# Decoder layer on one core: x1 of batches 1 to 3 transposed by DMA instead of TensorE

## The chip, the core and the metric

The kernel runs on one core of a Trainium2 chip. Its engines work side by side and wait for each other through semaphores: TensorE (PE) multiplies matrices and loads their stationary operands (PEld), VectorE (DVE), ScalarE (ACT) and GpSimd (POOL) work element by element, SyncE (SP) starts most of the DMAs. SBUF is the memory on the core, 128 partitions wide; PSUM holds TensorE's results. The metric is the time of one launch on the device in microseconds (us); lower is better. All times in the rows are counted from the start of the profiled span.

## The reference, cut to what matters

```
x1 = layernorm(x + attention_like(x))                       # (4, 512, 512) float32
xq = quant_dequant(x1)          # one scale for the whole tensor, rounded to fp8 (e4m3) values
cq = quant_dequant(ctx)
x2 = layernorm(x1 + einsum('bmk,bkn->bmn', xq, cq) + mask)  # the "cross" stage
mlp = silu(x2 @ gate_w) * (x2 @ up_w) @ down_w              # 512 -> 2048 -> 512
out = layernorm(x2 + mlp + experts(x2))                     # 8 of 1024 experts for each token
```

## The kernel before

There are 4 batches of 512 tokens; a batch is four tiles of 128 tokens by 512 features, tile i of batch b is `tile(4b + i)` of `xall`, which stays in SBUF in float32, tokens on partitions. Every stage writes its result over the same tile.

The program has two blocks. The first makes x1 for all batches and the scale of the quantisation. The second starts near 234 us; the change lies in its first 100 us.

**The cross stage.** `cross` multiplies the rounded x1 of a batch by the rounded ctx; the contraction runs over features, so the stationary operand has to have features on partitions. Before the change PE transposes x1 in float32 into the four PSUM banks gu0 to gu3 (function `transposes`, L1553; batch 0 in the first block), signals `x1t_mm`, and ACT copies each tile out of PSUM, multiplied by the scale, into `y_q` (`scaled`, L1187, signal `y_scaled`), and then writes a rounding magnitude `m_q` (L1189, signal `y_done`). DVE rounds with two instructions (`quantise`, L1293 and L1295) and writes bf16 values into `x_q`, already in the features' layout, signal `q_done`. PE's `cross` (L1561) waits for `q_done` of each tile.

**The mask.** POOL adds the mask to x1 by an accumulating DMA into `xall` (`add_mask`, L152). It may do this only when nobody needs x1 without the mask any more, so it waits for `x1t_mm` of that batch. POOL works in the order of its code: in turn n the addition for batch n + 2 stands between `low_h(n, 0)` and `power(n + 1)`, which makes rstd for the layernorm (L1102).

**x2 and the feed-forward product.** DVE adds the cross product to x1 (`residual`, L1303, L1305), finds the variance (L1310, L1312), and after POOL's rstd normalises (L1322). PE transposes x2 (the same `transposes`, signal `x2t_mm`), ACT and DVE split it into a high and a low part (L1195, L1328). The gate and up products use three PE products per pair of operands (L1541 to L1543), written in PSUM banks gu0, gu1 for the first half c = 0 of the hidden columns and gu2, gu3 for the second. ACT takes silu of gate (L1201), DVE multiplies by up (`middle`, L1334), ACT rounds (h_hi, L1207), POOL takes the remainder (h_lo, L1096), and PE makes the down product.

**The loop.** For n = 0, 1, 2 PE does: gate and up of batch n, half 0; cross of batch n + 1; the first eight transposes of x1 of batch n + 2; gate of half 1; the other eight; up of half 1; `down_early(n, 0)`; the sixteen transposes of x2 of batch n + 1; `down_early(n, 1)`. For n = 2 there is no batch n + 2 and no x1 transposes. Everything is written out by hand in this order; nothing reorders it when it runs. SP's order there is: store x2 of batch 0, load weights, store x2 of batch 1, load weights, and so on.

Of the kernel before, what the change touches and what calls it, by code (L numbers as in the profile page):

```python
# [16 lines left out]
BF16 = mybir.dt.bfloat16  # L17
I32 = mybir.dt.int32
U32 = mybir.dt.uint32
ALU = mybir.AluOpType  # L20
# [3 lines left out]
P = 128  # L24
B, S, D = 4, 512, 512
KC = D // P
# [63 lines left out]
def decoder_layer(nc, x, ctx, mask, w_in, b_in, w_out, b_out, gamma, beta, w_q, keys, down_embed, up_embed,  # L90
# [14 lines left out]
    with ExitStack() as whole:  # L105
        def sem(name):
            return whole.enter_context(nc.semaphore(name))
# [41 lines left out]
        def add_mask(b):  # L149

            nc.gpsimd.wait_ge(x1t_mm, TB * (b + 1))
            nc.gpsimd.dma_start(xall[:, b * TB * D:(b + 1) * TB * D].rearrange("p (t n) -> p t n", t=TB), mask[b, 0].partition_broadcast(P).unsqueeze(1).broadcast_to([P, TB, D]),  # L152
                                accum_op=ALU.add).then_inc(xm_in[b], 16)
# [5 lines left out]
        table_in = sem("table_in")  # L159
        x1t_mm = sem("x1t_mm")  # L160
        first_steps = []

        with ExitStack() as first:
# [69 lines left out]
            def tile(j):  # L233
                return xall[:, j * D:(j + 1) * D]
# [680 lines left out]
        with ExitStack() as second:  # L915
# [33 lines left out]
            m_q = [half[:, i * D:(i + 1) * D] for half in (scratch[:, 7 * D:8 * D].bitcast(BF16), x2_tok[0][:].bitcast(BF16)) for i in range(2)]  # L949
            x_q = scratch[:, 4 * D:6 * D].bitcast(BF16).rearrange("p (t c n) -> p t c n", t=TB, c=KC)  # L950
            ctx_f32 = ctx_q[:].bitcast(F32)
            qT = ctx_f32[:, 0:NT * P]
# [10 lines left out]
            def h_of(n):  # L963
                return h_end if n == UNITS - 1 else (h_hi, h_lo)

            key_in, x2_out, row_in, x2_in = sem("key_in"), [sem(f"x2_out{b}") for b in range(B)], sem("row_in"), [sem("x2_in0"), sem("x2_in1")]
            y_scaled, y_done, q_done, cross_mm, z2_done, v3_ready, r3_ready, x2_done, x2t_mm, h2_done, l2_done = (
                sem(n) for n in ("y_scaled", "y_done", "q_done", "cross_mm", "z2_done", "v3_ready", "r3_ready", "x2_done", "x2t_mm", "h2_done", "l2_done"))
            gate_mm, up_mm, silu_done, mid_done, hhi_done, hlo_done, down_mm, acc_done = (
                sem(n) for n in ("gate_mm", "up_mm", "silu_done", "mid_done", "hhi_done", "hlo_done", "down_mm", "acc_done"))  # L970
            query_mm, query_out, route_mm, route_out, soft_in, exp_done = (sem(n) for n in ("query_mm", "query_out", "route_mm", "route_out", "soft_in", "exp_done"))
            idx_ready, row_got, dot_done, gate_done, coef_done, pick_done = sem("idx_ready"), [sem(f"row_got{k}") for k in range(TOPK)], sem("dot_done"), sem("gate_done"), sem("coef_done"), sem("pick_done")
            key_zero, rows_clear = sem("key_zero"), sem("rows_clear")
            var_out, rstd_out, y_out, stored = sem("var_out"), sem("rstd_out"), sem("y_out"), sem("stored")
            block = second.enter_context(nc.Block())

            def tile(j):
                return xall[:, bass.ds(j * D, D)]

            def x1t_bank(b, i):  # L980

                return i if b < 2 else i % 2


# [23 lines left out]
            def _(sp):  # L1008
# [13 lines left out]
                def store_x2(b):  # L1022
                    sp.wait_ge(x2_done, TB * (b + 1))
                    sp.dma_start(x2_dram[:, b * TB * D:(b + 1) * TB * D], xall[:, b * TB * D:(b + 1) * TB * D]).then_inc(x2_out[b], 16)

                def load_x2(t):

                    if t >= 2:
                        sp.wait_ge(dot_done, (TOPK + 1) * (t - 1))
                    sp.dma_start(x2_tok[t % 2][:], x2_dram[:, t * D:(t + 1) * D]).then_inc(x2_in[t % 2], 16)  # L1030
# [7 lines left out]
                load(2, 0, 2)  # L1038
                load(3, 0, 3)
                store_x2(0)  # L1040
                load(4, 1, 0)
                store_x2(1)
                load(5, 1, 1)
                store_x2(2)
                load(6, 1, 2)
# [121 lines left out]
            def _(act):  # L1167
# [12 lines left out]
                def scaled(b, tiles):  # L1180
                    for i in tiles:

                        j = TB * b + i
                        act.wait_ge(x1t_mm, j + 1)
                        if j >= TB:
                            act.wait_ge(q_done, j - TB + 1)
                        nc.scalar.activation(y_q[i], gu[x1t_bank(b, i)][:], ACT.Copy, scale=scale_x[:, 0:1]).then_inc(y_scaled, 1)  # L1187
                        act.wait_ge(y_scaled, j + 1)
                        nc.scalar.activation(m_q[i], y_q[i], ACT.Abs, scale=ROUND_TO_4_BITS).then_inc(y_done, 1)  # L1189
# [91 lines left out]
            def _(dve):  # L1281
# [3 lines left out]
                def quantise(b, tiles):  # L1285
                    for i in tiles:
                        j = TB * b + i
                        y, m = y_q[i], m_q[i]

                        dve.wait_ge(y_done, j + 1)  # L1290
                        if b and i == 0:
                            dve.wait_ge(cross_mm, TB * b)
                        own.did(nc.vector.scalar_tensor_tensor(y, m, ROUND_SUBNORMAL, y, ALU.max, ALU.add))  # L1293
                        own.wait()
                        nc.vector.scalar_tensor_tensor(x_q[:, i].rearrange("p c n -> p (c n)"), m, ROUND_SUBNORMAL, y, ALU.max, ALU.subtract).then_inc(q_done, 1)  # L1295

# [242 lines left out]
            def _(pe):  # L1539
# [4 lines left out]

                def transposes(b, tiles, bank, count, free, ready=None):

                    for i in tiles:
                        free(i)
                        if ready is not None:
                            pe.wait_ge(ready, TB * b + i + 1)  # L1550
                        for c in range(KC):
                            j = TB * b + i
                            last = nc.tensor.transpose(gu[bank(i)][:, c * P:(c + 1) * P], xall[:, j * D + c * P:j * D + (c + 1) * P], ident[:])  # L1553
                        last.then_inc(count, 1)

                def cross(b, free):
                    for i in range(TB):
                        free(i)
                        pe.wait_ge(q_done, TB * b + i + 1)
                        for c in range(KC):  # L1560
                            last = nc.tensor.matmul(ob[i][:], x_q[:, i, c], ctx_q[:, (b * KC + c) * D:(b * KC + c + 1) * D], start=(c == 0), stop=(c == KC - 1))  # L1561
                        last.then_inc(cross_mm, 1)

                def gate_up(n, g_set, tb, c, w_loads, between=None):

# [6 lines left out]
                    last.then_inc(gate_mm, 1)  # L1572
                    if between is not None:
                        between()
                    if w_loads is not None:
# [29 lines left out]
                def freed(count, base):  # L1605
                    return lambda i: pe.wait_ge(count, base + i + 1)
# [3 lines left out]

                def own_bank(i):
                    return i

                def x1_bank(b):
                    return lambda i: x1t_bank(b, i)

                def first_half_free(n):
                    return lambda i: pe.wait_ge(mid_done, GC * n + 1)

                def x2_bank_free(n):  # L1620

                    def free(i):
                        if i >= 2:
                            pe.wait_ge(mid_done, GC * n + 2)
                        elif n + 2 < TB:
                            pe.wait_ge(y_done, TB * (n + 2) + 3 + i)
                        else:
                            pe.wait_ge(mid_done, GC * n + 1)
                    return free

                cross(0, nothing)
                transposes(1, range(TB), own_bank, x1t_mm, freed(y_done, 0))
                transposes(0, range(TB), own_bank, x2t_mm, freed(y_done, TB), x2_done)
                for n in range(TB - 1):
                    pe.wait_ge(l2_done, TB * (n + 1))
                    gate_up(n, 0, n, 0, 2 if n == 0 else None)
                    cross(n + 1, freed(acc_done, TB * (n - 1)) if n else freed(z2_done, 0))
                    if n + 2 < TB:
                        transposes(n + 2, (0, 1), x1_bank(n + 2), x1t_mm, first_half_free(n))
                        gate_up(n, 0, n, 1, None, lambda: transposes(n + 2, (2, 3), x1_bank(n + 2), x1t_mm, freed(y_done, TB * (n + 2) - 2)))  # L1640
                    else:
                        gate_up(n, 0, n, 1, None)
                    down_early(n, 0, freed(z2_done, TB * (n + 1)))
                    transposes(n + 1, range(TB), own_bank, x2t_mm, x2_bank_free(n), x2_done)
                    down_early(n, 1, nothing)
# [57 lines left out]
```

## Time and profile before

| | us |
|---|---|
| median of three runs | 830.55 |
| lowest and highest | 829.32, 830.72 |
| the profiled execution | 832.66 |
| its span, first to last instruction | 830.8 |

| engine | busy us | share of the span |
|---|---|---|
| PE | 783.0 | 94% |
| DVE | 683.5 | 82% |
| POOL | 369.6 | 44% |
| ACT | 298.9 | 36% |

The mean granted TensorE clock is 0.974 of full speed. A line of the profile that names an instruction gives its start, its duration, its engine, its line in the code, what it writes and reads, and in square brackets how long the engine sat idle before it and which instruction released it. The names are cut: `x_tok` is `x2_tok`, `x_hi` is `x2_hi`, `xall` is all the tiles. SPq is SP's queue of DMA issues.

### The profile page before, as it was taken

To read this page: it belongs to the slowest core of one execution; us is meant where nothing else is said; L and a number is where in the kernel's file an instruction comes from. 1 tells how busy PE (TensorE), PEld (TensorE's weight loads), DVE (VectorE), ACT (ScalarE), POOL (GpSimd) and SP (SyncE) were. 2 spreads that over 40 slices of the span, in tenths; PEclk is the share of its full clock that TensorE was granted. 3 is DMA by queue.
4 is the path that set the end of the run, shared out by engine and by line. 5 is a ranking of instruction groups with operands and counts; after the bars stand their busy time and mean duration, and the time that the engine had idled before them with its cause. 6 is when DMAs were issued, how large, how long until landed. Compare 5 with 4: busy or idle time off the path is not lost. (4 is left out here: it accounts for less than half of the span.)

```text
span 830.8 us, 10484 instructions
## 1 busy us (share of the span) xinstructions
PE 783.0 (94%) x3542; PEld 639.4 (77%) x3542; DVE 683.5 (82%) x1335; ACT 298.9 (36%) x665; POOL 369.6 (44%) x297
## 2 busy tenths in 40 slices
PE   8898999989749999999999999999999999999994
PEld 7776888877527778888888888888877877878783
DVE  5878589778889776057769999999999999999997
ACT  4542535353054342312163334233333333333320
POOL 1231121214213331212267776766667677676431
PEclk9999999998967999999999999999999999999998
DMA  8566514685324452000021331232332333222113
GB/s 323 209 135 169 102 52 102 134 271 102 52 66 127 127 127 102 26 1 31 29 61 50 116 94 47 79 94 65 96 103 83 99 90 109 65 86 73 34 77 126
DMA packets 51047, 81.69 MB, mean 98 GB/s; under 512 B 17488, under 2 KB 26448, under 8 KB 50481
## 3 DMA queue, kind: packets, MB, share of 16 engines
q0 software_dynamic: 24384, 33.48, 18.7%
q1 hardware_dynamic: 25024, 47.52, 16.3%
q8 instruction: 28, 0.46, 0.2%
q10 hardware_dynamic: 1584, 0.01, 0.1%
q14 instruction: 27, 0.21, 0.1%
HBM read 110.44 MB, written 12.58 MB: 148 GB/s over the span
## 5 line engine op out<-in xcount | busy, mean ns | idle before, releaser
L1541 PE MATMUL gu<-x_hi,w_hi 128*128 128x512 f32 x528 | 207.9, 394 | 3.5 <-DVE mid L1334 2.0
L1543 PE MATMUL gu<-x_hi,w_lo 128*128 128x512 f32 x528 | 206.4, 391 | 0.0
L1542 PE MATMUL gu<-x_lo,w_hi 128*128 128x512 f32 x528 | 206.3, 391 | 0.0
L1096 POOL TENSOR_TENSOR h_lo<-mid,h_hi 128x512 fp32r<-128x512 f32 x62 | 80.2, 1313 | 106.3 <-ACT h_hi L1207 105.9
L1541 PEld LDWEIGHTS gu<-x_hi,w_hi 128*128 128x128 f32 x528 | 99.7, 189 | 26.9 <-DVE mid L1334 4.6
L1543 PEld LDWEIGHTS gu<-x_hi,w_lo 128*128 128x128 f32 x528 | 99.6, 189 | 20.9
L1542 PEld LDWEIGHTS gu<-x_lo,w_hi 128*128 128x128 f32 x528 | 99.7, 189 | 20.2
L1217 ACT ACTIVATE gates<-dots 128x1 f32<-128x1 f32 x144 | 29.3, 203 | 232.1 <-DVE dots L1425 232.1
L1110 POOL DMA_INDIRECT ctx_q<-table_dram,row_i x64 | 79.9, 1249 | 63.1 <-DVE xall L1434 43.9
L1110 POOL DMA_INDIRECT scratch<-table_dram,row_i x64 | 82.4, 1287 | 39.8 <-issue 21.7
L1541 PE MATMUL ob<-w_hi,h_hi 128*128 128x512 f32 x248 | 97.5, 393 | 2.1 <-POOL h_lo L1096 2.1
L1334 DVE TENSOR_TENSOR mid<-gu,mid 128x512 f32<-128x512 f32 x64 | 44.2, 690 | 64.8 <-PE gu L1543 43.4
L1543 PE MATMUL ob<-w_hi,h_lo 128*128 128x512 f32 x248 | 96.6, 390 | 0.0
L1542 PE MATMUL ob<-w_lo,h_hi 128*128 128x512 f32 x248 | 96.6, 390 | 0.0
L1425 DVE CUSTOM_DVE_ANT_0 junk<-x_tok,scratch 128x512 bf16<-128x512 f32 x64 | 80.4, 1256 | 0.3
L1425 DVE CUSTOM_DVE_ANT_0 junk<-x_tok,ctx_q 128x512 bf16<-128x512 f32 x64 | 65.7, 1027 | 0.5
L1491 DVE TENSOR_TENSOR xall<-ob,xall 128x512 f32<-128x512 f32 x100 | 63.0, 682 | 2.3 <-PE ob L1543 0.3
L1091 POOL TENSOR_TENSOR w_lo<-xhat,w_hi 128x1024 fp32r<-128x1024 f32 (+1 forms) x23 | 55.1, 2397 | 20.3 <-ACT w_hi L1178 15.9
L1541 PEld LDWEIGHTS ob<-w_hi,h_hi 128*128 128x128 f32 x248 | 46.6, 188 | 13.7 <-POOL h_lo L1096 4.3
L1207 ACT ACTIVATE h_hi<-mid 128x512 fp32r<-128x512 f32 x62 | 36.0, 620 | 58.6 <-PE ob L1543 33.1
L1201 ACT ACTIVATE mid<-gu 128x512 f32<-128x512 f32 x64 | 37.3, 584 | 49.4 <-PE gu L1543 49.3
L1543 PEld LDWEIGHTS ob<-w_hi,h_lo 128*128 128x128 f32 x248 | 46.6, 188 | 9.8
(198 smaller groups left out, 1380.7 us busy)
## 6 DMA issues: line engine op xcount, KB each, us to landing
stage<-in_ctx SPq DMA_DIRECT2D x7, 1024.0 KB, 5.3
total<-prod POOLq DMA_DIRECT2D x12, 512.0 KB, 4.7
xall<-half_bo POOLq DMA_DIRECT2D x4, 1024.0 KB, 9.7
xhat<-in_L_ffn_gate_w SPq DMA_DIRECT2D x8, 512.0 KB, 3.7
xhat<-in_L_ffn_up_w SPq DMA_DIRECT2D x8, 512.0 KB, 3.3
xall<-in_mask_Bx1xS_ff POOLq DMA_DIRECT2D x4, 1024.0 KB, 10.7
xhat<-in_L_ffn_down_w SPq DMA_DIRECT2D x8, 512.0 KB, 3.4
x_dram<-xall SPq DMA_DIRECT2D x4, 1024.0 KB, 7.8
```

The costliest lines, as they stand in the source:

```text
L1091: nc.gpsimd.tensor_tensor(flat(lo, r), stage_of(r, slot), flat(hi, r).bitcast(F32), ALU.subtract).then_inc(wlo_done, 1)
L1096: nc.gpsimd.tensor_tensor(lo[:, c], mid[c][:], hi[:, c].bitcast(F32), ALU.subtract).then_inc(hlo_done, 1)
L1110: nc.gpsimd.indirect_dma_start(rows[k], None, table_dram[:, :], bass.IndirectOffsetOnAxis(ap=row_i[t % 2][:, k:k + 1], axis=0), bounds_che ...
L1201: nc.scalar.activation(mid[c][:], gu[2 * c][:], ACT.Silu).then_inc(silu_done, 1)
L1207: nc.scalar.activation(h_of(n)[0][:, c], mid[c][:], ACT.Copy).then_inc(hhi_done, 1)
L1217: nc.scalar.activation(gates[:, t % 2, k:k + 1], dots[:, t % 2, k:k + 1], ACT.Silu).then_inc(gate_done, 1)
L1334: nc.vector.tensor_tensor(mid[c][:], gu[2 * c + 1][:], mid[c][:], ALU.mult).then_inc(mid_done, 1)
L1425: nc.vector.tensor_tensor_reduce(out=junk2[:], in0=x2_tok[par][:], in1=row[:, 0:D], scale=1.0, scalar=0.0, op0=ALU.mult, op1=ALU.add, accu ...
L1491: nc.vector.tensor_tensor(tile(j), ob[i][:], tile(j), ALU.add).then_inc(acc_done, 1)
L1541: nc.tensor.matmul(dst, lhs[0], rhs[0], start=start, stop=False)
L1542: nc.tensor.matmul(dst, lhs[0], rhs[1], start=False, stop=False)
L1543: return nc.tensor.matmul(dst, lhs[1], rhs[0], start=False, stop=stop)
```

## The change

The rounding of batches 1 to 3 is done in the tokens' layout. ACT's `scaled` reads the tile of `xall` directly and no longer waits for a transpose. DVE writes the bf16 result into a new buffer `q_tok[i]` (one per tile, in `scratch` and `x2_tok[1]`), and SP starts four DMA transposes of 128 by 128 for each tile, from `q_tok[i]` into `x_q`, each adding 16 to `xq_in[i]`. PE's `cross` waits for `xq_in[i]` where it waited for `q_done`. The x1 transposes of batches 1 to 3 on PE are gone; those of batch 0 stay. DVE's rounding from batch 2 on waits until the tile's transposes of the batch before have landed, and `add_mask` of batches 1 to 3 waits for `y_scaled`.

```
 def add_mask(b):
-    nc.gpsimd.wait_ge(x1t_mm, TB * (b + 1))
+    if b:
+        nc.gpsimd.wait_ge(y_scaled, TB * (b + 1))
+    else:
+        nc.gpsimd.wait_ge(x1t_mm, TB)
...
+q_tok = [half[:, i * D:(i + 1) * D] for half in (scratch[:, 6 * D:7 * D].bitcast(BF16), x2_tok[1][:].bitcast(BF16)) for i in range(2)]
...
+def transpose_q(b):                                       # SP
+    for i in range(TB):
+        sp.wait_ge(q_done, TB * b + i + 1)
+        sp.wait_ge(cross_mm, TB * (b - 1) + i + 1)
+        for c in range(KC):
+            sp.dma_start_transpose(x_q[:, i, c], q_tok[i][:, c * P:(c + 1) * P]).then_inc(xq_in[i], 16)
...
 load(3, 0, 3)
+transpose_q(1)
 store_x2(0)
 load(4, 1, 0)
+transpose_q(2)
 store_x2(1)
 load(5, 1, 1)
+transpose_q(3)
 store_x2(2)
...
 # ACT, scaled(b, tiles)
-act.wait_ge(x1t_mm, j + 1)
-if j >= TB:
+if b:
     act.wait_ge(q_done, j - TB + 1)
-nc.scalar.activation(y_q[i], gu[x1t_bank(b, i)][:], ACT.Copy, scale=scale_x[:, 0:1]).then_inc(y_scaled, 1)
+else:
+    act.wait_ge(x1t_mm, j + 1)
+nc.scalar.activation(y_q[i], tile(j) if b else gu[i][:], ACT.Copy, scale=scale_x[:, 0:1]).then_inc(y_scaled, 1)
...
 # DVE, quantise(b, tiles)
-if b and i == 0:
-    dve.wait_ge(cross_mm, TB * b)
+if b >= 2:
+    dve.wait_ge(xq_in[i], 16 * KC * (b - 1))
...
-nc.vector.scalar_tensor_tensor(x_q[:, i].rearrange("p c n -> p (c n)"), m, ROUND_SUBNORMAL, y, ALU.max, ALU.subtract).then_inc(q_done, 1)
+nc.vector.scalar_tensor_tensor(q_tok[i] if b else x_q[:, i].rearrange("p c n -> p (c n)"), m, ROUND_SUBNORMAL, y, ALU.max, ALU.subtract).then_inc(q_done, 1)
...
 # PE, cross(b, free)
-pe.wait_ge(q_done, TB * b + i + 1)
+if b:
+    pe.wait_ge(xq_in[i], 16 * KC * b)
+else:
+    pe.wait_ge(q_done, i + 1)
...
+def unit_half_read(n):
+    return lambda i: pe.wait_ge(mid_done, GC * n + i // 2 + 1)
...
 cross(0, nothing)
-transposes(1, range(TB), own_bank, x1t_mm, freed(y_done, 0))
-transposes(0, range(TB), own_bank, x2t_mm, freed(y_done, TB), x2_done)
+transposes(0, x2t_mm, freed(y_done, 0), x2_done)
 for n in range(TB - 1):
     pe.wait_ge(l2_done, TB * (n + 1))
     gate_up(n, 0, n, 0, 2 if n == 0 else None)
     cross(n + 1, freed(acc_done, TB * (n - 1)) if n else freed(z2_done, 0))
-    if n + 2 < TB:
-        transposes(n + 2, (0, 1), x1_bank(n + 2), x1t_mm, first_half_free(n))
-        gate_up(n, 0, n, 1, None, lambda: transposes(n + 2, (2, 3), x1_bank(n + 2), x1t_mm, freed(y_done, TB * (n + 2) - 2)))
-    else:
-        gate_up(n, 0, n, 1, None)
+    gate_up(n, 0, n, 1, None)
     down_early(n, 0, freed(z2_done, TB * (n + 1)))
-    transposes(n + 1, range(TB), own_bank, x2t_mm, x2_bank_free(n), x2_done)
+    transposes(n + 1, x2t_mm, unit_half_read(n), x2_done)
     down_early(n, 1, nothing)
```

PE's program order at the end of the cross product in the loop, before; `ctx_q,scratch` are the cross products of tiles 2 and 3 (the rounded x1 lies in `scratch`), `ident,xall` the x1 transposes of the next batch, `x2_hi,w_hi` the gate product of half 1:

```order
L1561 MATMUL ob2<-ctx_q,scratch 128x512 [waits q_done,z2_done]
L1561 MATMUL ob2<-ctx_q,scratch 128x512 x3
L1561 MATMUL ob3<-ctx_q,scratch 128x512 [waits q_done,z2_done]
L1561 MATMUL ob3<-ctx_q,scratch 128x512 x3
L1553 MATMUL gu0<-ident,xall 128x128 [waits mid_done]
L1553 MATMUL gu0<-ident,xall 128x128 x3
L1553 MATMUL gu1<-ident,xall 128x128 [waits mid_done]
L1553 MATMUL gu1<-ident,xall 128x128 x3
L1541 MATMUL gu2<-x2_hi,w_hi 128x512
```

And PE at the same place in the changed program:

```order
L1576 MATMUL ob2<-ctx_q,scratch 128x512 [waits xq_in2,z2_done]
L1576 MATMUL ob2<-ctx_q,scratch 128x512 x3
L1576 MATMUL ob3<-ctx_q,scratch 128x512 [waits xq_in3,z2_done]
L1576 MATMUL ob3<-ctx_q,scratch 128x512 x3
L1553 MATMUL gu2<-x2_hi,w_hi 128x512
```

The gate product follows the cross product directly, and each tile of the cross product waits for its own DMA semaphore. Eight more transposes are gone between the gate and the up product.

SP's program order after the loads at the start of the second block, before; `x2_dram<-xall` is a store of x2, `xhat<-...` a load of weights:

```order
L1018 DMA xhat<-in_L0_ffn_down_w 128x2x512 [waits wlo_done,whi_done]
L1016 DMA xhat<-in_L0_ffn_W_q 128x4x128 [waits wlo_done,whi_done]
L1024 DMA x2_dram<-xall 128x2048 [waits x2_done]
L1020 DMA xhat<-in_L0_ffn_gate_w 128x4x256 [waits wlo_done,whi_done]
L1024 DMA x2_dram<-xall 128x2048 [waits x2_done]
```

And SP in the changed program, from the same load of W_q on; `scratch<-scratch` and `scratch<-x2_tok1` are transposes from `q_tok` into `x_q`:

```order
L1017 DMA xhat<-in_L0_ffn_W_q 128x4x128 [waits wlo_done,whi_done]
L1032 DMA_TRANSPOSE scratch<-scratch 128x128 [waits cross_mm,q_done]
L1032 DMA_TRANSPOSE scratch<-scratch 128x128 x3
L1032 DMA_TRANSPOSE scratch<-scratch 128x128 [waits cross_mm,q_done]
L1032 DMA_TRANSPOSE scratch<-scratch 128x128 x3
L1032 DMA_TRANSPOSE scratch<-x2_tok1 128x128 [waits cross_mm,q_done]
L1032 DMA_TRANSPOSE scratch<-x2_tok1 128x128 x3
L1032 DMA_TRANSPOSE scratch<-x2_tok1 128x128 [waits cross_mm,q_done]
L1032 DMA_TRANSPOSE scratch<-x2_tok1 128x128 x3
L1025 DMA x2_dram<-xall 128x2048 [waits x2_done]
L1021 DMA xhat<-in_L0_ffn_gate_w 128x4x256 [waits wlo_done,whi_done]
```

The first store of x2 and the load behind it stand behind sixteen transposes, each group of four behind the rounding of its tile.

POOL's order in the first turn of the loop is the same in both programs; what changes is the semaphore of the mask addition, ahead of rstd:

```order
L1107 TENSOR_TENSOR h_lo<-mid0,h_hi 128x512 [waits hhi_done]
L155 DMA xall<-in_mask_Bx1xS2_ff0 128x4x512 [waits y_scaled]
L1113 TENSOR_TENSOR rstd2<-var2,neg_half 128x4 [waits x2_done,v3_ready]
L1107 TENSOR_TENSOR h_lo<-mid1,h_hi 128x512 [waits hhi_done]
L1102 TENSOR_TENSOR w_lo<-xhat,w_hi 128x1024 [waits whi_done]
```

Before, the addition's row reads `[waits x1t_mm]`.

## Rows read from the trace of the kernel before

**Rows 1.** Busy time by stretch: start:end, length, engines' busy us, PEclk, DMA share, GB/s

```profile
261.70:285.90 24.20, 23.66 (x121) 18.39 (x120) 19.29 (x35) 10.29 (x17) 7.72 (x5) 1.00 0.43 109
326.25:345.00 18.75, 18.75 (x84) 15.56 (x83) 2.35 (x4) 4.66 (x7) 3.12 (x2) 1.00 0.23 76
```

**Rows 2.** PE's timeline ahead of the loop: start, duration, instruction, idle and releaser

```profile
242.50 1.91 PE L1553 MATMUL gu<-ident,xall 128*128 128x128 f32 x16
249.13 3.65 PE L1553 MATMUL gu<-ident,xall 128*128 128x128 f32 x16 [4.72 <-DVE xall L1322]
```

**Rows 3.** PE's timeline in the first turn, and the next cross product

```profile
261.71 3.63 PE L1561 MATMUL ob<-ctx_q,scratch 128*128 128x512 bf16 x16
265.18 1.04 PE L1553 MATMUL gu<-ident,xall 128*128 128x128 f32 x8
265.97 0.47 PE L1541 MATMUL gu<-x_hi,w_hi 128*128 128x512 f32 x1
266.28 0.39 PE L1542 MATMUL gu<-x_lo,w_hi 128*128 128x512 f32 x1
...
277.61 0.50 PE L1541 MATMUL ob<-w_hi,h_hi 128*128 128x512 f32 x1 [0.54 <-POOL h_lo L1096]
...
285.91 3.63 PE L1561 MATMUL ob<-ctx_q,scratch 128*128 128x512 bf16 x16
```

**Rows 4.** POOL's timeline in the first turn

```profile
270.17 1.32 POOL L152 DMA_DIRECT2D xall<-in_mask_Bx1xS_ff  x1 [5.49 <-PE gu L1553]
271.00 1.55 POOL L1102 TENSOR_TENSOR rstd<-var,neg_half 128x4 f32<-128x4 f32 x1
```

**Rows 5.** ACT's timeline in the first turn: silu of half 1, last scaling copy

```profile
269.02 0.60 ACT L1201 ACTIVATE mid<-gu 128x512 f32<-128x512 f32 x1 [0.61 <-PE gu L1543]
...
270.77 0.67 ACT L1187 ACTIVATE scratch<-gu,scale_x 128x512 f32<-128x512 f32 x1
```

**Rows 6.** DVE's timeline in the first turn: variance, normalise, second mid product

```profile
268.86 0.17 DVE L1312 TENSOR_SCALAR var<-mv 128x4 f32<-128x4 f32 x1
...
272.58 1.92 DVE L1322 TENSOR_SCALAR xall<-xall,mv,rstd 128x512 f32<-128x512 f32 x4 [2.22 <-POOL rstd L1102]
274.42 0.68 DVE L1334 TENSOR_TENSOR mid<-gu,mid 128x512 f32<-128x512 f32 x1
```

**Rows 7.** DVE's timeline: roundings of batch 1 (tiles 1, 2, 3), batch 2 (2, 3)

```profile
254.77 2.75 DVE L1295 SCALAR_TENSOR_TENSOR scratch<-scratch 128x512 bf16<-128x512 bf16 x1
...
259.24 0.69 DVE L1295 SCALAR_TENSOR_TENSOR scratch<-x_tok,scratch 128x512 bf16<-128x512 bf16 x1
...
260.57 0.69 DVE L1295 SCALAR_TENSOR_TENSOR scratch<-x_tok,scratch 128x512 bf16<-128x512 bf16 x1
...
281.54 0.69 DVE L1295 SCALAR_TENSOR_TENSOR scratch<-x_tok,scratch 128x512 bf16<-128x512 bf16 x1
...
284.07 0.69 DVE L1295 SCALAR_TENSOR_TENSOR scratch<-x_tok,scratch 128x512 bf16<-128x512 bf16 x1
```

**Rows 8.** SP's timeline of DMA issues: keys, first store of x2

```profile
234.25 2.42 SPq L1035 DMA_DIRECT2D key_sb<-in_L_ffn_keys  x4
...
250.51 0.34 SPq L1024 DMA_DIRECT2D x_dram<-xall  x1
```

**Rows 9.** DMA issues from 225 to 345: count, KB each, median us to landing

```profile
x_dram<-xall SPq DMA_DIRECT2D x4, 1024.0 KB, 7.8
...
x_tok<-x_dram SPq DMA_DIRECT2D x2, 256.0 KB, 3.0
...
key_sb<-in_L_ffn_keys SPq DMA_DIRECT2D x4, 16.0 KB, 2.0
```

**Rows 10.** A gap on PE in the first block (timeline), and the clock around it

```profile
187.29 0.80 PE L756 MATMUL ob<-xn_hi,w_hi 128*128 128x512 f32 x1 [2.86 <-ACT qT L420]
...
184.00:188.00 4.00, 1.14 (x4) 0.62 (x4) 2.97 (x6) 2.78 (x7) 0.69 (x2) 0.84 0.07 27
188.00:192.00 4.00, 4.00 (x15) 3.18 (x14) 2.67 (x6) 2.05 (x3) 1.09 (x3) 0.74 0.71 135
```

More of the change, by code:

```diff
@@ L159, in decoder_layer @@
         table_in = sem("table_in")
-        x1t_mm = sem("x1t_mm")
+        x1t_mm, y_scaled = sem("x1t_mm"), sem("y_scaled")
         first_steps = []
@@ L966, in decoder_layer @@
             key_in, x2_out, row_in, x2_in = sem("key_in"), [sem(f"x2_out{b}") for b in range(B)], sem("row_in"), [sem("x2_in0"), sem("x2_in1")]
-            y_scaled, y_done, q_done, cross_mm, z2_done, v3_ready, r3_ready, x2_done, x2t_mm, h2_done, l2_done = (
-                sem(n) for n in ("y_scaled", "y_done", "q_done", "cross_mm", "z2_done", "v3_ready", "r3_ready", "x2_done", "x2t_mm", "h2_done", "l2_done"))
+            y_done, q_done, cross_mm, z2_done, v3_ready, r3_ready, x2_done, x2t_mm, h2_done, l2_done = (
+                sem(n) for n in ("y_done", "q_done", "cross_mm", "z2_done", "v3_ready", "r3_ready", "x2_done", "x2t_mm", "h2_done", "l2_done"))
             gate_mm, up_mm, silu_done, mid_done, hhi_done, hlo_done, down_mm, acc_done = (
@@ L972, in decoder_layer @@
             idx_ready, row_got, dot_done, gate_done, coef_done, pick_done = sem("idx_ready"), [sem(f"row_got{k}") for k in range(TOPK)], sem("dot_done"), sem("gate_done"), sem("coef_done"), sem("pick_done")
+            xq_in = [sem(f"xq_in{i}") for i in range(TB)]
             key_zero, rows_clear = sem("key_zero"), sem("rows_clear")
@@ L978, in tile @@
                 return xall[:, bass.ds(j * D, D)]
-            def x1t_bank(b, i):
-                return i if b < 2 else i % 2
             def load_index(g, r):
@@ L1543, in three, with transposes @@
                     return nc.tensor.matmul(dst, lhs[1], rhs[0], start=False, stop=stop)
-                def transposes(b, tiles, bank, count, free, ready=None):
-                    for i in tiles:
+                def transposes(b, count, free, ready=None):
+                    for i in range(TB):
                         free(i)
@@ L1552, in transposes @@
                             j = TB * b + i
-                            last = nc.tensor.transpose(gu[bank(i)][:, c * P:(c + 1) * P], xall[:, j * D + c * P:j * D + (c + 1) * P], ident[:])
+                            last = nc.tensor.transpose(gu[i][:, c * P:(c + 1) * P], xall[:, j * D + c * P:j * D + (c + 1) * P], ident[:])
                         last.then_inc(count, 1)
@@ L1562, in cross, with gate_up @@
                         last.then_inc(cross_mm, 1)
-                def gate_up(n, g_set, tb, c, w_loads, between=None):
+                def gate_up(n, g_set, tb, c, w_loads):
                     cols = slice(tb * S, (tb + 1) * S)
@@ L1572, in gate_up @@
                     last.then_inc(gate_mm, 1)
-                    if between is not None:
-                        between()
                     if w_loads is not None:
@@ L1609, in nothing @@
                     pass
[L1611 to L1626, printed above, removed]
-                        else:
-                            pe.wait_ge(mid_done, GC * n + 1)
-                    return free
+                def unit_half_read(n):
+                    return lambda i: pe.wait_ge(mid_done, GC * n + i // 2 + 1)
                 cross(0, nothing)
-                transposes(1, range(TB), own_bank, x1t_mm, freed(y_done, 0))
-                transposes(0, range(TB), own_bank, x2t_mm, freed(y_done, TB), x2_done)
+                transposes(0, x2t_mm, freed(y_done, 0), x2_done)
                 for n in range(TB - 1):
@@ L1637, in _ @@
                     cross(n + 1, freed(acc_done, TB * (n - 1)) if n else freed(z2_done, 0))
-                    if n + 2 < TB:
-                        transposes(n + 2, (0, 1), x1_bank(n + 2), x1t_mm, first_half_free(n))
-                        gate_up(n, 0, n, 1, None, lambda: transposes(n + 2, (2, 3), x1_bank(n + 2), x1t_mm, freed(y_done, TB * (n + 2) - 2)))
-                    else:
-                        gate_up(n, 0, n, 1, None)
+                    gate_up(n, 0, n, 1, None)
                     down_early(n, 0, freed(z2_done, TB * (n + 1)))
-                    transposes(n + 1, range(TB), own_bank, x2t_mm, x2_bank_free(n), x2_done)
+                    transposes(n + 1, x2t_mm, unit_half_read(n), x2_done)
                     down_early(n, 1, nothing)
```

## The prediction

> **What bounds the kernel now.** I read the busy table by stage first. In the stage of the change [rows 1] TensorE (PE) is busy 23.66 of 24.20 us at clock 1.00, VectorE (DVE) 19.29, ScalarE (ACT) 10.29, GpSimd (POOL) 7.72. One turn of the loop over n, from the cross product of batch 1 at 261.71 to that of batch 2 at 285.91, takes exactly these 24.20 us; the next turn repeats it to the hundredth. From 326.25 to 345 PE has no gap at all, so a delay that arrives there is carried to the end. Read alone, this says: what PE no longer does is gained. The second view, PE's instructions in order [rows 3], has the one line that speaks against it: at 277.61 the second half of the down product starts after 0.54 us of idle time, released by h_lo. Between two cross products there is one place where PE is not the bound.
>
> That wait is the end of a chain, read backwards through POOL, ACT and DVE [rows 4 to 6]: h_lo on POOL, the second mid product (DVE 274.42), normalise (DVE 272.58), rstd (POOL 271.00), and in front of rstd on POOL's own queue the issue of the mask addition (270.17), which had waited for the x1 transposes of the next batch. The variance that rstd needs was ready on DVE by 269.03, so rstd is held about 2 us by the mask's wait. From the start of the cross product to 277.61 the chain takes 15.90 us. Removing PE work between these two points can give back 0.54 us at most, unless the chain gets shorter too.
>
> **What is removed.** Eight transposes move the next product from 265.18 to 265.97, 0.79 us, and this product takes 0.47 instead of 0.39 [rows 3]: 0.88 us for eight. Batches 2 and 3 have sixteen each, 1.76 us a turn, 3.5 us for both. Batch 1's sixteen lie at 242.50 to 244.41, ahead of 4.72 us in which PE waits for x2 [rows 2]: removed from idle time, worth nothing. There ACT may now scale batch 1 some 4 us earlier; nobody on the path waits for that, since DVE goes on with the residual of batch 0 either way.
>
> **What happens to the chain (the mask).** The mask addition overwrites x1, so it now waits for all four scaling copies of ACT, y_scaled, instead of PE's transposes, x1t_mm. In ACT's order the last two copies stand behind silu of the second half. Before, that silu starts at 269.02 and the last copy at 270.77, ending 271.44: 2.42 us after the silu [rows 5]. The gate product now ends 0.88 earlier (the first eight transposes are gone), so silu starts at 268.14 and the last copy ends at 270.56; the mask, which started at 270.17, starts at 270.64 (0.08 for the signal, my estimate; ACT to POOL is the tightest handover seen). The chain becomes 0.47 longer. PE saves 1.76, then waits 1.76 + 0.54 + 0.47 = 2.8 us in place of 0.54. Per turn: +0.47, for n = 0 and n = 1: +0.94. The last turn has no next batch.
>
> **What the DMA transposes cost.** Each tile is four transposes issued one after another by SP, then the landing, and only then may the cross product of this tile start. The trace before has no such transfer. The bounds for an issue: 0.34 us (SP's store of x2) below, 1.32 us (POOL's mask addition) above; the nearest row in size is the load of the keys, 64 rows of 256 bytes, four in 2.42 us, 0.6 each [rows 8]. I take 0.6. For the landing: 2.0 (16 KB) and 3.0 (256 KB) [rows 9]; a transpose moves 32 KB, I take 2.5 from its issue.
> Batch 1: DVE's rounding ends at 257.52, 259.93 and 261.26 for tiles 1, 2, 3 [rows 7]. SP needs 2.4 a tile: tile 1 is issued by 260.0, tile 2 by 262.4, tile 3 has its last issue at 264.2 and lands at 266.7. PE wants tile 3 at 261.71 + 3 x 0.87 = 264.3 (0.87 from 3.47 us for four tiles). Wait: 2.4 us.
> Batch 2: tiles 2 and 3 are rounded at 282.23 and 284.76 [rows 7]; tile 3 is issued from 284.8 to 286.6, lands at 289.1, and is wanted at 285.91 + 2.6 = 288.5: 0.6. The rounding waits for PE's down product there, so both ends move together. Batch 3 has the same rows 24.2 us later: 0.6. In all 3.6 us. It adds fully: the gate product, the silu, the copies and the mask of the same turn stand behind the last tile. With issues of 0.34 and landings of 2.0 the sum is 0; with 1.32 it is 21 (below).
>
> **What else is moved on SP.** The stores of x2 and the loads of the next weights now stand behind sixteen transposes. The first store goes from 250.51 to about 265, the load behind it to about 265.4. The store's first reader is DVE's accumulation of the down product, whose second half starts at 277.61 [rows 3]; 1 MB lands in 7.8 us: time is left. The load's reader on ACT stands behind h_hi of the second half, so after the mid product of 274.42; the load is half the size of the store [rows 9] and queued behind it, so it lands by about 274. Covered, with 1 to 2 us to spare; if this cover goes, x2_hi and the next gate product are late by as much.
>
> **The clock.** PE's new wait of 2.8 us a turn is broken only by transposes. In the trace before, a gap of 2.86 us ahead of 187.29 is followed by the half clock: PEclk is 0.84 in 184 to 188 and 0.74 in 188 to 192 [rows 10]. The second is 2.1 us at 1.2 GHz, and with 0.7 us of the first some 2.8 us after the gap, which cost 1.4 us of PE time. Whether the transposes inside the new wait keep the clock up no row shows. I count the 1.4 us in both turns: +2.8. The stage runs at clock 1.00 before [rows 1], so below this term is 0.
>
> **The sum.** 0.94 (longer chain, after PE's 3.5 us have gone into the wait) + 3.6 (landing of the transposes) + 2.8 (clock) = +7.3 us. The profiled execution took 832.66 us around a span of 830.8; it would be 840.0. The three runs have a median of 830.55, 2.1 lower, so I forecast 837.9.
>
> **Rivals.**
> Slow transposes. If SP needs 1.32 us each, a tile takes 5.3: batch 1 is issued by 262.9, 268.2 and 273.4, its last tile lands at 274.6 against 264.3, 10.3 us. Batches 2 and 3: tile 2 from 282.3, tile 3's last issue at 291.5, landing at 294.0 against 288.5, 5.5 each. That is 21.3 + 0.94, and five gaps at 1.4 us: +29, 860; without the clock 853. I put it at 856. For it: a transposed tile is no plain copy, and issues made in software cost 1.32 already. Against it: every SP row here is 0.6 or less.
> The Trainium skill (VectorE: DVE Perf Modes, section "The three transpose paths") gives 1309 ns for a 128x128 bf16 transpose by DMA and 390 ns on TensorE; if these come one after another the sum is this rival's. The Trainium skill (Advanced Engine Details and Errata, section "X-Bar Transpose (TRN2)") says that such DMAs are as fast as regular ones, which would be my forecast's side. No row of before decides between the two pages.
> Hidden transposes. Issues of 0.34 to 0.5 and landings of 2.0 end before PE asks, and the clock holds: only the 0.94 stays, 831.5, or 832 with part of a wait. For it: tiles 0 and 1 have several us in hand in every batch. Against: tile 3 of batch 1 is rounded only 0.45 us before the cross product starts.
> Faster. PE's 3.5 us come through: 827.0. For that rstd must start at 271.00 - 1.76 = 269.24 or earlier, so the mask at 268.4 or earlier; the variance at 269.03 would allow it, ACT's order does not, since two copies (2.4 us) stand behind a silu that starts at 268.1. It decides only if the copies end before 268.4 and the tiles land in time.
> Much worse: queued behind mask and store traffic, or transposes dearer than any row: above 862.
>
> **How the numbers follow.** Forecast 0.42, slow transposes 0.30, hidden 0.12, faster 0.07, much worse 0.09. A measurement of this kernel can tell 0.2%, 1.7 us, from no change: the forecast, the slow and the much worse case lie above it, the hidden case within, the faster case below. Slower 0.81, same 0.12, faster 0.07. The range leaves out the faster and the much worse case: 831 to 861.
>
> **What would show it.** Right: the down product's second half waits for h_lo near 2.8 us in each of the first two turns; the mask's issue follows ACT's last copy; cross products wait for DMA, longest in batch 1; PEclk below 1.00 between 262 and 310; identical rows after 326 moved as a block. Wrong: a turn still of 24.2 us or shorter (the chain was not the bound), cross products without a wait, or SP issues near or over 1.3 us (then the slow rival).

## The result and the profile after

The changed kernel takes 858.64 us (median of 4 runs, 858.55 to 858.67) against 830.63 for the kernel before (829.32 to 832.82): ratio 1.0334, 95% interval 1.0312 to 1.0356. It is slower by 28 us where I had forecast 7.3. The time lies inside the stated range, 2.6 us above the 856 of the case that I had called slow transposes (853 to 860 had been worked out for it), which I had given 0.30.

The stage by itself, in the busy table of the changed kernel (start:end, length, busy us of PE, PEld, DVE, ACT, POOL, PEclk, DMA share, GB/s):

```profile
262.00:266.00 4.00, 1.87 (x4) 0.43 (x4) 1.46 (x3) 1.80 (x3) 0.63 (x1) 0.56 0.12 25
266.00:270.00 4.00, 1.87 (x4) 0.43 (x4) 0.53 (x1) 0.00 (x0) 0.00 (x0) 0.50 0.12 25
...
300.00:304.00 4.00, 0.23 (x2) 0.00 (x0) 1.94 (x3) 0.80 (x2) 0.00 (x0) 0.93 0.12 25
304.00:308.00 4.00, 3.32 (x8) 2.08 (x9) 1.38 (x2) 0.00 (x0) 0.00 (x0) 0.50 0.88 263
```

Where [rows 1] had every engine at work, hardly any is busy here, the DMA engines least of all: 12% and 25 GB/s in three of the four stretches, while PE waits for a DMA. With the DMA engines this idle, the next place to look is the engine that issues the transfers. SP's queue of issues, the counterpart of [rows 8]:

```profile
247.02 14.20 SPq L1032 DMA_TRANSPOSE scratch<-scratch  x8
261.32 10.10 SPq L1032 DMA_TRANSPOSE scratch<-x_tok  x8
271.47 0.58 SPq L1025 DMA_DIRECT2D x_dram<-xall  x1
```

Eight transposes for tiles 2 and 3 take 10.10 us without a pause. The view of this line gives the time of one issue (min/median/max, ns) and the landing:

```profile
L1032 SPq DMA_TRANSPOSE scratch<-scratch x24: 1094/1232/2677, 247.0 to 324.3; - x24
L1032 SPq DMA_TRANSPOSE scratch<-x_tok x24: 1094/1233/1236, 261.3 to 334.8; - x24
...
DMA to landing us min/median/max: 2.2/2.3/8.5
```

PE's timeline, the counterpart of [rows 3]; L1576 is the cross product, L1565 the transposes of x2, L1553 with `ob<-w_hi,h_hi` the down product's second half:

```profile
258.51 1.04 PE L1576 MATMUL ob<-ctx_q,scratch 128*128 128x512 bf16 x4
...
262.47 1.87 PE L1576 MATMUL ob<-ctx_q,scratch 128*128 128x512 bf16 x4 [2.93 <-DMA scratch<-scratch]
...
267.57 1.87 PE L1576 MATMUL ob<-ctx_q,scratch 128*128 128x512 bf16 x4 [3.23 <-DMA scratch<-x_tok]
...
272.67 1.86 PE L1576 MATMUL ob<-ctx_q,scratch 128*128 128x512 bf16 x4 [3.23 <-DMA scratch<-x_tok]
...
284.00 1.08 PE L1565 MATMUL gu<-ident,xall 128*128 128x128 f32 x8 [0.50 <-DVE xall L1334]
...
285.88 1.09 PE L1565 MATMUL gu<-ident,xall 128*128 128x128 f32 x8 [0.79 <-DVE mid L1346]
...
288.33 0.50 PE L1553 MATMUL ob<-w_hi,h_hi 128*128 128x512 f32 x1 [1.35 <-POOL h_lo L1107]
...
296.67 1.90 PE L1576 MATMUL ob<-ctx_q,scratch 128*128 128x512 bf16 x8
...
304.68 1.86 PE L1576 MATMUL ob<-ctx_q,scratch 128*128 128x512 bf16 x4 [4.45 <-DMA scratch<-x_tok]
...
329.61 1.90 PE L1576 MATMUL ob<-ctx_q,scratch 128*128 128x512 bf16 x8
...
337.23 1.59 PE L1576 MATMUL ob<-ctx_q,scratch 128*128 128x512 bf16 x4 [4.08 <-DMA scratch<-x_tok]
```

Three things are to be seen. The tiles of batch 1 start 5.10 us apart, SP's pace of four issues. A quarter of the cross product takes 1.86 us at tile 3 where it takes 1.04 at tile 0: the clock has fallen in the waits (PEclk 0.50 from 266 to 270). And the second half of the down product now waits in three pieces, 0.50 + 0.79 + 1.35 = 2.64 us, where it waited 0.54. This longer wait has its cause in ACT and POOL, counterparts of [rows 5] and [rows 4]:

```profile
278.10 0.60 ACT L1213 ACTIVATE mid<-gu 128x512 f32<-128x512 f32 x1 [14.27 <-PE gu L1555]
...
279.88 0.71 ACT L1199 ACTIVATE scratch<-xall,scale_x 128x512 f32<-128x512 f32 x1
```

```profile
280.89 1.32 POOL L155 DMA_DIRECT2D xall<-in_mask_Bx1xS_ff  x1 [18.26 <-ACT scratch L1199]
281.72 1.55 POOL L1113 TENSOR_TENSOR rstd<-var,neg_half 128x4 f32<-128x4 f32 x1
```

The mask's issue now names ACT's scaling copy as its releaser, 0.30 us after the last copy's end, and rstd stands behind it, as foreseen.

Three points in a turn split it by cause: the start of the cross product's tile 3, the silu of half 1, and the down product's second half. Against the kernel before (tile 3 at 2.6 us after the cross product's start, silu and down product from [rows 5] and [rows 3]; the last turn was read in the same way):

| us longer than before | turn 0 | turn 1 | turn 2 | sum |
|---|---|---|---|---|
| cross start to tile 3 (landing) | 11.56 | 5.41 | 5.02 | 22.0 |
| tile 3 to silu of half 1 | 0.72 | 1.72 | 1.63 | 4.1 |
| silu to down product, second half | 1.64 | 1.63 | 0.03 | 3.3 |
| down product to next cross start | 0.04 | -0.02 | | 0.0 |

Together 29.4 us. The second line is the sum of two things: the clock costs 5.8 us there (worked out below), and the eight x1 transposes that stood between tile 3 and the silu are gone from turns 0 and 1, 0.88 us each.

The loop began 3.2 us earlier in this execution. 1.3 us of it lie in the first block, whose code the change leaves alone. 1.9 lie in the first gate and up products, which ran at the full clock from their start at 252.93 where the kernel before ran at the half clock until 258. Whether the change has a part in that is open: in the traces of all the kernels here these products took 5.6 us in three, all of them without the x1 transposes, and 7 to 8.7 in the others, with and without them. It made no difference to the time, since tile 3 had to wait for SP anyway: these 1.9 us went into its 11.56. 29.4 - 3.2 is 26.2; the spans differ by 25.8.

### The profile page after: what moved, and what is told of

It reads as the page before. It is cut to its first block and busy times, and to the rows that moved or that the text cites. A ratio compares the mean times of both kernels' runs of the same rounds, so it can differ in the third digit from the quotient of the medians.

```text
span 856.6 us, 10441 instructions
## 1 busy us (share of the span) xinstructions
PE 782.3 (91%) x3494; PEld 633.7 (74%) x3494; DVE 684.1 (80%) x1335; ACT 298.7 (35%) x665; POOL 369.9 (43%) x297
## 3 DMA queue, kind: packets, MB, share of 16 engines
q0 software_dynamic: 24384, 33.48, 18.4%
## 5 line engine op out<-in xcount | busy, mean ns | idle before, releaser
L1553 PE MATMUL gu<-x_hi,w_hi 128*128 128x512 f32 x528 | 209.1, 396 | 3.1 <-DVE mid L1346 1.7
L1553 PEld LDWEIGHTS gu<-x_hi,w_hi 128*128 128x128 f32 x528 | 100.4, 190 | 27.3 <-DVE mid L1346 4.2
L1553 PE MATMUL ob<-w_hi,h_hi 128*128 128x512 f32 x248 | 97.4, 393 | 3.7 <-POOL h_lo L1107 3.7
L1553 PEld LDWEIGHTS ob<-w_hi,h_hi 128*128 128x128 f32 x248 | 46.6, 188 | 15.3 <-POOL h_lo L1107 5.9
```

What stands on the lines that cost most here:

```text
L1553: nc.tensor.matmul(dst, lhs[0], rhs[0], start=start, stop=False)
```

## The experiments

Theory S: SP's issue of a DMA transpose, 1.23 us where I took 0.6, times four a tile, is most of the loss. The rivals: that any DMA between the rounding and the cross product costs this (landing, order, mask); that the clock or the mask's chain carries it.

**Plain copies in place of transposes.**

```
-sp.dma_start_transpose(x_q[:, i, c], q_tok[i][:, c * P:(c + 1) * P]).then_inc(xq_in[i], 16)
+sp.dma_start(x_q[:, i, c], q_tok[i][:, c * P:(c + 1) * P]).then_inc(xq_in[i], 16)
```

> SP starts four plain DMA copies per tile, same size and same places, where the changed kernel starts four DMA transposes; the transposition itself is left out. Theory (SP's issue of a transpose, 1.23 us each and one after another, is most of the 28 us): plain issues near 0.5 us, cross products wait 3 to 4 us in batch 1 and under 0.5 in batches 2 and 3, time 833 to 838. Rival (any DMA between rounding and cross product costs this, through landing, order and mask): 845 to 858.

Measured: 838.61 us against 831.25 (ratio 1.0078, 1.0055 to 1.0101). The issues, and their landing:

```profile
L1032 SPq DMA_DIRECT2D scratch<-scratch x24: 465/598/663, 248.4 to 308.6; - x24
L1032 SPq DMA_DIRECT2D scratch<-x_tok x24: 465/602/624, 260.2 to 317.2; - x24
...
DMA to landing us min/median/max: 1.7/1.8/8.2
```

Same bytes, same places, same order, 0.60 us an issue: 20 us of the 28 are gone, theory S stands. The landing is shorter as well, by 0.5 us, which is little beside it. The time is half a microsecond above the range that I had written for it. It is the case that my forecast had really worked out (0.6 an issue, 837.9). The closeness is in part luck: in this trace, by the same split as above, the waits for the DMAs are 4.5 us (forecast 3.6), the longer chain 1.5 (0.94) and the clock 3.5 (2.8), and the loop began 1.8 us earlier than before.

**Half of the transposes.**

```
-for c in range(KC):
+for c in range(2):
     sp.dma_start_transpose(x_q[:, i, c], q_tok[i][:, c * P:(c + 1) * P]).then_inc(xq_in[i], 16)
```

(with the waits on `xq_in[i]` halved)

> Only two of the four 128x128 blocks of each tile are transposed; the other two are left out of the cross product's input. Theory (SP's issues one after another): 2.5 us a tile instead of 5.1, tile 3 of batch 1 is issued 5.1 to 7 us earlier, batches 2 and 3 hardly wait: cross products wait about 6 us in batch 1 and 0 to 0.5 in batches 2 and 3 (22 us in all now), time 836 to 841. Rival (a fixed price of the DMA path and of the order): time above 850.

Measured: 836.99 us (1.0065, 1.0044 to 1.0085). The issues keep their price (median 1.18 to 1.20 us), and there are half as many: the tiles of batch 1 start 2.55 us apart instead of 5.10, batches 2 and 3 don't wait at all. Batch 1 waits 3.9 us, less than the 6 that I had expected. The waits shrink with the number of issues, not with a fixed price of the path.

**One transpose for a whole tile.**

```
-for c in range(KC):
-    sp.dma_start_transpose(x_q[:, i, c], q_tok[i][:, c * P:(c + 1) * P]).then_inc(xq_in[i], 16)
+sp.dma_start_transpose(x_q[:, i], q_tok[i]).then_inc(xq_in[i], 16)
```

(with the waits on `xq_in[i]` divided by four)

> One DMA transpose of 128x512 per tile in place of four of 128x128, the same layout in x_q. If the 1.23 us are a price per instruction: about 1.3 us a tile, time 832 to 838. If they are a price per 128x128 block of data: 5 us a tile as now, time 857 to 860. In between if a fixed part is saved four times.

Measured: 833.88 us (1.0028, 1.0012 to 1.0043).

```profile
L1031 SPq DMA_TRANSPOSE scratch<-scratch x6: 1190/1194/1302, 246.7 to 301.8; - x6
L1031 SPq DMA_TRANSPOSE scratch<-x_tok x6: 1189/1190/1192, 258.4 to 310.1; - x6
...
DMA to landing us min/median/max: 2.4/2.4/5.0
```

A transpose of 128x512 is issued in 1.19 us, one of 128x128 in 1.23: the price is one per instruction and does not depend on the size here. Nor is it a wait for the transfer before: in the changed kernel the transpose issued at 278.03, more than 5 us after SP's last issue, took 1.09 us too. The landing is 0.1 us later. PE waits for no transpose any more:

```profile
259.74 3.63 PE L1575 MATMUL ob<-ctx_q,scratch 128*128 128x512 bf16 x16
...
276.37 0.73 PE L1552 MATMUL ob<-w_hi,h_hi 128*128 128x512 f32 x1 [1.35 <-POOL h_lo L1106]
286.29 3.63 PE L1575 MATMUL ob<-ctx_q,scratch 128*128 128x512 bf16 x16
...
302.92 0.50 PE L1552 MATMUL ob<-w_hi,h_hi 128*128 128x512 f32 x1 [1.36 <-POOL h_lo L1106]
311.25 3.63 PE L1575 MATMUL ob<-ctx_q,scratch 128*128 128x512 bf16 x16
```

What is left is the prediction's first term and, in one of the two turns, its clock term. From cross product to second half it is 16.63 us in both turns, 0.73 more than the 15.90 of before (forecast 0.47), though PE does 1.76 us less. The second turn is 24.96 us long; the first is 26.55, because its down product starts at the half clock (0.73 us for its first product instead of 0.50), which costs 1.6 us up to the next cross product: the same gap of 0.50 + 0.79 + 1.35 us cost the clock once and spared it once.

**The clock.** Idle products in front of the waits; their results are overwritten by the cross product.

```
 # PE, cross(b, free)
 if b:
+    for _ in range(FILL[b][i]):      # FILL = {1: (0, 12, 18, 18), 2: (0, 0, 2, 20), 3: (0, 0, 2, 18)}
+        nc.tensor.matmul(ob[i][:], ctx_q[:, 0:P], ctx_q[:, 0:D], start=True, stop=True)
     pe.wait_ge(xq_in[i], 16 * KC * b)
```

> The changed kernel with idle products on TensorE (12, 18, 18 ahead of tiles 1 to 3 of batch 1, 2 and 20 ahead of tiles 2 and 3 of batch 2, 2 and 18 in batch 3), placed in front of the waits for the transposes, their results overwritten. Theory (the clock falls in these waits and costs 4 to 6 us behind them): PEclk stays at 1.00 from 262 to 345, time 853 to 855. Rival (the clock costs nothing, the chain on DVE, ACT and POOL hides it): 858.6, or more if the products outlast the waits.

Measured: 855.90 us (853.42 to 857.63; 1.0294, 1.0276 to 1.0313). That is 2.7 less than the changed kernel's median, or 3.3 if each is counted from the runs of the kernel before beside it. Two rows of its busy table, then PE at tile 3 of batch 1 and at the down product's second half behind it:

```profile
262.00:282.00 20.00, 19.95 (x92) 11.56 (x92) 7.83 (x16) 6.19 (x10) 2.40 (x3) 1.00 0.34 98
282.00:300.00 18.00, 15.28 (x68) 11.26 (x68) 12.91 (x22) 5.10 (x9) 5.59 (x5) 0.91 0.46 78
...
274.27 1.04 PE L1580 MATMUL ob<-ctx_q,scratch 128*128 128x512 bf16 x4
...
288.32 0.80 PE L1553 MATMUL ob<-w_hi,h_hi 128*128 128x512 f32 x1 [1.35 <-POOL h_lo L1107]
```

PEclk is 1.00 where the changed kernel has 0.66 in the same 20 us. From tile 3 to the silu of half 1 it is 3.82 or 3.83 us in all three turns, against 5.43, 6.42 and 5.44: the clock had cost 1.6 + 2.6 + 1.6 = 5.8 us. The time gained less, and the trace shows most of the difference. The second block began 1.3 us later in this execution. Tile 3 of batch 1 started at 274.27, 1.6 us later than in the changed kernel: these 1.3, and 0.3 because SP issued the transposes of tiles 2 and 3 in 10.49 us instead of 10.10. And in turn 0 the clock fell in the gap ahead of the down product instead (0.91), where nothing was filled in, which cost 1.4 us. The idle products themselves held nothing up: in each batch tile 3 starts 1.1 to 1.3 us after the end of SP's last issue, with them and without. The theory was right in its mechanism; of what I expected, the time (853 to 855) was too low by 1 us, and the clock did not stay at 1.00 up to 345.

**The mask's wait alone, on the kernel before.**

```
-nc.gpsimd.wait_ge(x1t_mm, TB * (b + 1))
+nc.gpsimd.wait_ge(y_scaled if b else x1t_mm, TB * (b + 1))
```

> The kernel before, TensorE's transposes kept, only the mask addition of batches 1 to 3 waits for ACT's four scaling copies instead of the transposes. Theory: the mask's issue moves from 270.17 to about 271.7, the chain is 1.6 us longer in each of two turns, PE waits 2.1 us where it waited 0.54: +3.1 us, 833.7; with a fall of the clock up to 836.5. Rival (the mask's wait is covered): no change.

Measured: 835.40 us against 831.15 (1.0059, 1.0045 to 1.0072), +4.3. The traced execution was the fastest of the five, 833.91 us, +2.8. In its trace the turns are 25.80 and 25.76 us long, 1.6 more than 24.20, at PEclk 1.00:

```profile
274.75 1.09 PE L1553 MATMUL gu<-ident,xall 128*128 128x128 f32 x8 [0.54 <-DVE mid L1334]
...
277.20 0.50 PE L1541 MATMUL ob<-w_hi,h_hi 128*128 128x512 f32 x1 [1.35 <-POOL h_lo L1096]
```

One semaphore on POOL's queue, on an engine busy 7.7 of 24.2 us, costs 1.6 us a turn. That is 3.2 us for two turns; what the slower executions lost beyond it I can't say, since none of them has a trace.

**rstd ahead of the mask**, on the changed kernel and on the kernel before.

```
-if n + 2 < TB:
-    add_mask(n + 2)
 if n + 1 < TB:
     power(n + 1)
+if n + 2 < TB:
+    add_mask(n + 2)
```

> The changed kernel with rstd ahead of the mask addition on POOL. Theory: between silu of half 1 and the down product's second half the chain loses the mask; rstd starts at the variance, some 4 to 5 us earlier in turns 0 and 1, and PE is the bound there: PE's 2.6 us of idle time per turn vanish, 5.3 us in all, 853.4. Rival (the wait for the transposes alone decides): no change, 858.6.

Measured: 852.63 us (1.0270, 1.0255 to 1.0284), 6.0 less than the changed kernel's median. PE's three gaps are gone in both turns, 5.3 us together; the first turn:

```profile
283.58 1.91 PE L1565 MATMUL gu<-ident,xall 128*128 128x128 f32 x16
285.24 0.48 PE L1553 MATMUL ob<-w_hi,h_hi 128*128 128x512 f32 x1
```

The chain's share of the loss, 1.5 us, and PE's removed transposes, 3.5 us, which had been lost in it, come back together.

> The kernel before with one exchange on POOL: rstd (power) of batch n+1 stands ahead of the mask addition of batch n+2. Theory (in the kernel before, rstd is held 2 us by the mask's wait, and this chain ends in PE's 0.54 us of idle time ahead of the down product's second half): both idle times of 0.54 us vanish, 829.4, a gain of 1.1 us. Rival (the 0.54 has another releaser): no change.

Measured: 831.17 against 831.15 (0.9995, 0.9986 to 1.0005). The trace has both turns at 23.40 us instead of 24.20 and no gap ahead of the down product, so 1.6 us less; the timed runs allow a gain of 1.2 us at most. They fall in two groups: five at 829.05 to 829.80 us with a mean granted clock of 0.976, the traced one among them, and six at 831.17 to 832.06 us with 0.973 or 0.974. The first group has about the gain of the trace, the second does not. What the second lost, and where, stays open, as it has no trace.

**Both together: a version that beats both kernels.** One transpose per tile, and rstd ahead of the mask.

> One DMA transpose per tile (128x512), and on POOL rstd ahead of the mask addition. With one transpose per tile the turn of the loop took 24.96 us in the trace where the clock held (24.20 before), all of it in the chain through the mask. Theory (only the mask's place keeps the kernel from the gain of PE's removed transposes): rstd starts 2 to 3 us earlier, the turn falls to 22 to 22.4 us, PE's gap of 0.5 + 0.8 + 1.35 us shrinks below 0.5, 827 to 828 against 831.2 before. Rival (another link of the chain or the landing of the transposes takes its place): 830 to 834.

Measured: 827.27 us against 831.78 (0.9943, 0.9930 to 0.9956).

```profile
260.41 3.40 PE L1575 MATMUL ob<-ctx_q,scratch 128*128 128x512 bf16 x15
...
274.18 0.50 PE L1552 MATMUL ob<-w_hi,h_hi 128*128 128x512 f32 x1 [0.43 <-POOL h_lo L1106]
...
282.71 3.40 PE L1575 MATMUL ob<-ctx_q,scratch 128*128 128x512 bf16 x15
```

The turn is 22.30 us, 1.90 less than before; two of them make 3.8 of the 4.5 us. PE still waits 0.43 us for h_lo.

The same with POOL's order kept, and ACT's copies moved instead:

```
 if n + 2 < TB:
-    scaled(n + 2, (0, 1))
+    scaled(n + 2, range(TB))
 silu(n, 1)
-if n + 2 < TB:
-    scaled(n + 2, (2, 3))
```

> One DMA transpose per tile; POOL's order as in the changed kernel (mask addition, then rstd), but ACT makes all four scaling copies of the next batch ahead of silu of half 1. Theory (what lengthens the chain is that two copies stand behind this silu): the mask is issued at once when POOL reaches it, rstd starts at the variance plus the mask's 0.8 us, the turn is 22.6 to 23.2 us, 828 to 830. Rival (the mask's own issue on POOL or the moved silu costs as much): 832 to 835.

Measured: 827.93 us (0.9952, 0.9938 to 0.9966), turns of 22.16 and 22.20 us, both a little below what I had expected. Either end of the mask's wait may be moved, with the same gain. Both intervals lie below 1 and overlap.

## Why the prediction was wrong

**The step that failed: "the nearest row in size is the load of the keys ... 0.6 each. I take 0.6."** The term for the landing was forecast at 3.6 us and measured at 22.0. The waits follow from the prediction's own working once SP's measured pace is put in. With 5.10 us a tile in place of 2.4, and a landing of 2.3 us, it gives waits of 9.5, 5.0 and 5.0 us; the trace has 11.6, 5.4 and 5.0. The extra in batch 1 is mostly the earlier start of its cross product, 3.2 us, while DVE's rounding of tile 1 ended only 1.3 us earlier (256.27 against 257.52). So the mechanism was the one described, and its size was read from the wrong row: a plain copy of the same bytes does take 0.60 us, a transpose twice that, and the trace before held no transpose. The landing, 2.3 us, was near the 2.5 taken. I had the right sum written down as a rival (10.3, 5.5 and 5.5 us for 1.32 an issue) and gave the forecast to the cheaper row because it came from the same queue. The sign that I had named for that rival, SP issues near 1.3 us, is what the trace shows.

Term by term, the sum 0.94 + 3.6 + 2.8 = 7.3 us was measured as 1.5 + 22.0 + 5.8 = 29.3, in an execution whose loop began 3.2 us earlier. Of the difference, 18.4 us are the landing term, 3.0 the clock and 0.6 the chain.

The Trainium skill (VectorE: DVE Perf Modes, section "The three transpose paths") has 1309 ns for a 128x128 bf16 transpose by DMA; the trace's 1.23 us an issue is close to it (2.3 us up to the landing), but 128x512 takes 1.19, so here the figure belongs to the instruction and not to a block of this size. The other statement cited from the Trainium skill, that a transpose is as fast as a regular DMA (Advanced Engine Details and Errata, section "X-Bar Transpose (TRN2)"), does not hold for these small transfers: 1.23 against 0.60 us for the issue, 2.3 against 1.8 up to the landing.

**The mask's chain: right, and the reason for no gain.** Forecast 0.47 us a turn longer, measured 0.76 in the changed kernel and 0.73 with one transpose per tile. The missing 0.29 are the handover from ACT to POOL (0.30 us, not 0.08) and slower copies (0.71 us from SBUF, 0.67 before from PSUM). Forecast gap 2.8 us, measured 2.64; the 0.29 don't show in it, mostly because PE's sixteen transposes of x2, which ran in 1.91 us, now run in two groups of 1.08 and 1.09. PE's 3.5 us went into this gap, as said.

**The clock: right in kind, 2.8 forecast, 5.8 measured, at other places.** I had put it behind the gaps at the down product; in the changed kernel it fell in the longer waits for the transposes, three times, and not in these gaps. In the kernel with one transpose per tile it did fall in one of the two.

**Batch 1's transposes: worth nothing, as said.** They stood in idle time: the wait for x2 ahead of the loop is 7.20 us now where it was 4.72.

**SP's stores and loads behind the transposes: covered, as said.** The first store was issued at 271.47 instead of 250.51, and neither DVE's accumulation nor ACT's rounding of weights has a wait for a DMA in the changed kernel between 236 and 355. The rival of transposes that queue behind other traffic showed in one place: of the first three, issued from 247.02 to 249.5 beside the mask's transfer, two landed after 7.4 and 8.5 us, while PE wanted that tile only at 258.51.

## What to carry to other kernels

Ask of every DMA that is put on a path what its issue costs the issuing engine, and count instructions before you count bytes: sixteen issues of 1.23 us are 20 us of SP in a turn of 24, while transposes four times as large, a quarter as many, made PE wait for none. When work is taken from the busiest engine, look for the one place in the loop where it already waits, even for half a microsecond, and follow that chain back through the idle engines' queues; an order on one of these (here a mask's issue ahead of rstd) can hold the whole gain. An operation of a kind that the trace does not hold is better forecast by both ends with their chances than by the friendliest neighbouring row.

## What was not expected of the hardware

A DMA transpose of 128x512 bf16 from SBUF to SBUF is issued by SP in 1.19 us and lands 2.4 us after its issue, one of 128x128 in 1.23 and 2.3, a plain copy of 128x128 in 0.60 and 1.8. While SP issued transposes without a pause, the DMA engines were busy 12% at 25 GB/s. The same gap on PE, 2.64 us in three pieces, was followed by the half clock in one turn and by the full clock in the next of one execution.
